# Convolution branches rotated over four column groups of TensorE, small products on three of them

## What is computed

```python
specs = [(w1, 0, 1), (w2, 6, 6), (w3, 12, 12), (w4, 18, 18)]        # weights, pad, dilation; w1 is 1x1, the others 3x3
branches = [_bn_relu(_conv(x, w, p, d), ...) for i, (w, p, d) in enumerate(specs)]   # 32 channels each
x_q = jnp.concatenate(branches, axis=1)
Q = einsum('oi,bihw->bohw', wq, x_q) + bq        # 16 rows
K = einsum('oi,bihw->bohw', wk, x) + bk          # 16 rows
V = einsum('oi,bihw->bohw', wv, x) + bv          # 128 rows
Qn = _l2n(Q).transpose(0, 2, 1)
Kn = _l2n(K)
tailor = 1.0 / (N + einsum('bnm,bm->bn', Qn, Kn.sum(-1) + EPS))
mat = einsum('bmn,bcn->bmc', Kn, V)
msum = V.sum(-1)[:, :, None] + einsum('bnm,bmc->bcn', Qn, mat)
out = gamma * (msum * tailor[:, None, :])
```

## Time and profile before

| | us |
|---|---|
| median of 3 runs | 16281.83 |
| lowest and highest | 16277.56, 16301.75 |
| the profiled execution | 16276.23 |
| its span | 16274.4 |
| PE busy in the span | 14161.2 (87%) |
| DVE, POOL, ACT busy | 13974.3, 13069.0, 10107.5 |
| mean granted clock of TensorE | 0.925 |

### The profile page before, as it was taken

The page is one execution under the profiler, slowest core; times in us unless marked ns, Lnnn a source line. Parts: engine busy times, 40 slices in busy tenths (PEclk is TensorE's granted clock), DMA queues, the critical chain, the costliest instruction groups (busy, mean ns, idle before and its releaser), DMA issues. The chain is left out here.

```text
span 16274.4 us, 144588 instructions
## 1 busy us (share of the span) xinstructions
PE 14161.2 (87%) x40704; PEld 5407.5 (33%) x40704; DVE 13974.3 (86%) x13537; ACT 10107.5 (62%) x14054; POOL 13069.0 (80%) x5647
## 2 busy tenths in 40 slices
PE   8999997888888888888888888888888888888886
PEld 3333332333333333333333333333333333333332
DVE  1222228999999999999999999999999999999997
ACT  2222225666666666666666666666666676666675
POOL 0000007999999999999999999999999999999996
PEclk9999998999999999999999999999999999999997
DMA  1111104444445545444455454454544444545544
GB/s 50 42 39 44 39 26 151 171 161 169 170 172 180 180 168 180 173 178 171 175 182 181 168 180 173 176 182 164 182 178 172 177 176 175 182 167 181 180 173 172
DMA packets 560359, 2505.37 MB, mean 154 GB/s; under 512 B 58695, under 2 KB 171063, under 8 KB 293448
## 3 DMA queue, kind: packets, MB, share of 16 engines
q1 hardware_dynamic: 549272, 2477.68, 42.9%
q10 hardware_dynamic: 10288, 18.44, 0.4%
HBM read 2325.32 MB, written 170.57 MB: 153 GB/s over the span
## 5 line engine op out<-in xcount | busy, mean ns | idle before, releaser
L794 POOL TENSOR_TENSOR hc<-h,c_all 128x1024 f32<-128x1024 f32 x4096 | 9531.7, 2359 | 574.0 <-DVE h L1161 496.1
L1031 PE MATMUL y_ps<-hc,ident 128*128 128x512 f32 x16392 | 8392.7, 664 | 1127.8 <-POOL hc L794 1127.6
L892 ACT ACTIVATE d_a<-dt,a_neg 128x512 f32<-128x512 f32 x8194 | 5596.1, 689 | 4081.4 <-DVE h L1161 4055.4
L1161 DVE TENSOR_TENSOR_SCAN h<-d_a,h,dbx_v 128x512 f32<-128x512 f32 x5456 | 6622.0, 1262 | 10.4 <-DVE dbx_v L1148 1.1
L1031 PEld LDWEIGHTS y_ps<-hc,ident 128*128 128x128 f32 x16392 | 3362.3, 211 | 6055.1 <-issue 4172.5
L1148 DVE TENSOR_TENSOR dbx_v<-dtx_ps,b_all 128x1024 f32<-128x1024 f32 x2816 | 3313.7, 1206 | 61.0 <-issue 26.2
L1161 DVE TENSOR_TENSOR_SCAN h<-d_a,h,dbx_p 128x512 f32<-128x512 f32 x2480 | 3027.7, 1262 | 10.8 <-issue 0.4
L783 POOL TENSOR_TENSOR dbx_p<-dtx,b_all 128x1024 f32<-128x1024 f32 x1280 | 3002.3, 2355 | 23.8 <-DVE h L1161 0.8
L480 POOL MEMSET ident_f<- 128x128 f32 x1 | 0.2, 205 | 2417.5 <-POOLq L45 2417.5
L273 PE MATMUL conv_ps<-image,w_taps 128*32 128x512 f32 x11520 | 1777.7, 594 | 0.0
L363 DVE RECIPROCAL k_inv<-k_nrm 128x4 f32<-128x4 f32 x256 | 45.5, 178 | 1774.2 <-ACT k_nrm L215 1774.2
(11 more groups left out here) (143 smaller groups left out, 9228.5 us busy)
## 6 DMA issues: line engine op xcount, KB each, us to landing
b_all<-bc_dram SPq DMA_DIRECT2D x1028, 1024.0 KB, 6.3
c_all<-bc_dram SPq DMA_DIRECT2D x1025, 1024.0 KB, 5.0
o_dram<-o_sb SPq DMA_DIRECT2D x257, 256.0 KB, 6.2
o_c<-o_dram SPq DMA_DIRECT2D x220, 256.0 KB
out<-r_c SPq DMA_DIRECT2D x220, 256.0 KB, 7.9
image<-in_x SPq DMA_DIRECT2D x91, 512.0 KB, 4.1
un<-un_dram SPq DMA_DIRECT2D x736, 34.0 KB
bc_dram<-low_bc SPq DMA_DIRECT2D x257, 64.0 KB, 4.6
```

What stands on the lines that cost most here:

```text
L794: nc.gpsimd.tensor_tensor(hc[:, n % HC], h[:, n], c_all[:, n // CG % 2, n % CG].unsqueeze(1).broadcast_to([128, 2, CH]), ALU.mult).then_in ...
L892: nc.scalar.activation(d_a[:, half], dt[:, p, half], ACT.Exp, scale=a_neg[:, half, n:n + 1]).then_inc(a_done, 1)
L1031: last = nc.tensor.matmul(y_ps[:, half], ident[:], hc[:, n % HC, half], start=False, stop=(n == S - 1))
L1161: nc.vector.tensor_tensor_scan(h[:, n, half], d_a[:, half], dbx, zero_col[:] if first else h[:, n, half, CH - 1:CH], ALU.mult, ALU.add).th ...
```

## The change

- The branches no longer have fixed column groups. Chunk r's 1x1 branch is on group r mod 4 and the dilated ones on the three groups behind it, in turn. Weights for the center are laid down twice in a row (8 x 32 columns), so that a window of it gives the turned order; the query weights and the batch norm's constants come in four turned copies.
- `query` is on group 0, `query_norm` on group 1, `outer` on group 2 (`small_ps` holds all three), and group 3 has none of them.
- The order of PE's work on an image is made by a planner (`batch`) when the kernel is built. It goes in rounds: in each, every group gets one matmul in turn (group 2 four outer products at once), a small product if it is due, or else its next tap. A tap's chunk may be up to three ahead of the oldest unfinished one. A center is put just before the first tap of its chunk, wherever in the round that is, and kv at the start of a round.
- `conv_ps` has four banks, `x_q` two; Q and its sum of squares have two each.
- ACT does relu of chunk k, norms of k+1, then `length` (root and stores) of k-2 and `query` (copy and square) of k-1.
- POOL clears only the margins of `image`; the first loads don't wait for the clearing. PE waits for each quarter of the first image, and for the last 24 rows of later ones at chunk 20.

```diff
-        conv_ps = ps("conv_ps", [128, 2, CH])
+        conv_ps = ps("conv_ps", [128, 4, CH])
         kv_ps = ps("kv_ps", [128, 2, CH])
-        mat_ps = ps("mat_ps", [KU, 2, CH])
-        qs_ps = ps("qs_ps", [128, CH])
-        s_ps = ps("s_ps", [128, CH])
+        small_ps = ps("small_ps", [128, 2, CH])
+        qs_ps, s_ps, mat_ps = small_ps[0:M], small_ps[32:64], small_ps[64:64 + KU]
...
-            sp.wait_ge(cleared, 6)
             for i in range(4):
                 rows = slice(i * 32, i * 32 + 32)
                 sp.dma_start(image[:, PAD + 32 * i:PAD + 32 * i + 32, PAD:PAD + W],
-                             t["x"][0, :, rows, :]).then_inc(x_loaded, 16)
-
+                             t["x"][0, :, rows, :]).then_inc(x_first[i], 16)
+
+            sp.wait_ge(cleared, CLEARED)
...
-        def loaded(eng, b):
-
-            eng.wait_ge(x_loaded, 16 * 4 + b * (16 * (PIECES - 2)))
+        def loaded(eng, b, r):
+
+            if b == 0:
+                for i in range(4):
+                    if r == max(0, (32 * i - max(DIL) - ROWS) // ROWS):
+                        eng.wait_ge(x_first[i], 16)
+            elif r == 0:
+                eng.wait_ge(x_loaded, 16 * b * (PIECES - 3))
+            elif r == ((PIECES - 3) * PIECE - max(DIL) - ROWS) // ROWS:
+                eng.wait_ge(x_rest, 16 * b)
...
-            pool.memset(image[:], 0.0).then_inc(cleared, 1)
+            pool.memset(image[:, 0:PAD], 0.0).then_inc(cleared, 1)
+            pool.memset(image[:, PAD:PAD + H, 0:PAD], 0.0).then_inc(cleared, 1)
+            pool.memset(image[:, PAD:PAD + H, PAD + W:WP], 0.0).then_inc(cleared, 1)
+            pool.memset(image[:, PAD + H:WP], 0.0).then_inc(cleared, 1)
...
+                norms(b * NCH)
+                for r in range(NCH):
+                    k = b * NCH + r
+                    relu(k)
+                    if r + 1 < NCH:
+                        norms(k + 1)
+                    if r >= 2:
+                        length(k - 2)
+                    if r >= 1:
+                        query(k - 1)
+                k = b * NCH + NCH - 1
+                length(k - 1)
+                query(k)
+                length(k)
...
+            def center(k, r):
+                if k >= 4:
+                    pe.wait_ge(bn_done, k - 3)
+                y0, turn = r * ROWS + PAD, (4 - r % 4) % 4 * BR
+                nc.tensor.matmul(conv_ps[:, k % 4], w_center[:, turn:turn + 4 * BR],
+                                 image[:, y0:y0 + ROWS, PAD:PAD + W], start=True, stop=False, skip_group_check=True)
+
+            def tap(k, r, n, group):
+                i = (group - r) % 4 - 1
...
+                while min(queries, norms, outers) < NCH:
+                    if (keyed < min(begun + 1, NCH, outers + 3) and now >= keys_at.get(keyed - 1, -far) + 5
+                            and (keyed < 3 or now >= done_at.get(keyed - 3, far) + 4)):
+                        loaded(pe, b, keyed)
+                        kv(b * NCH + keyed, keyed)
+                        keys_at[keyed] = now
+                        keyed += 1
+                    for g in range(4):
+                        if g == 0 and now >= done_at.get(queries, far) + 3:
+                            query(b * NCH + queries, queries)
+                            query_at[queries] = now
+                            queries += 1
+                        elif g == 1 and now >= max(query_at.get(norms, far), done_at.get(min(norms + 1, NCH - 1), far)) + 4:
+                            query_norm(b * NCH + norms)
+                            norms += 1
+                        elif g == 2 and now >= max(keys_at.get(outers, far), done_at.get(outers - 1, far) if outers else 0) + 6:
+                            for j in range(SUB):
+                                outer(b * NCH + outers, j)
+                            outers += 1
+                        elif waiting[g] and waiting[g][0][0] <= told + 3:
+                            r, n = waiting[g].pop(0)
+                            for c in range(begun, r + 1):
+                                if keyed <= c:
+                                    loaded(pe, b, c)
+                                center(b * NCH + c, c)
+                            begun = max(begun, r + 1)
+                            left[r] -= 1
+                            if left[r] == 0:
+                                done_at[r] = now
+                            ended = 0
+                            while told + ended < NCH and left[told + ended] == 0:
+                                ended += 1
+                            told += ended
+                            last = tap(b * NCH + r, r, n, g)
+                            if ended:
+                                last.then_inc(conv_done, ended)
+                    now += 1
```

More of the change, by code:

```diff
@@ L35 @@
 PIECES = H // PIECE
+CLEARED = 9
 HC = 4
@@ L329, in _ @@
+            for b in range(B):
+                batch(b)
         @block.vector
```

201 lines of the change are left out of this document (88 added, 113 removed).

## The result

Measured in turn on one chip: after 16401.2 us (median; 16390.4 to 16412.4), before 16286.0 us (16277.6 to 16301.8). The ratio is 1.0070, 95% interval 1.0052 to 1.0087: slower by 115 us. The forecast was +47, 16329 us, and its range ended at 16390. The direction held; the time is outside the range, and the slowdown is more than twice the forecast.

The account below looks back on a forecast made before the run. PE was taken to bound the first stage, busy 289.4 of the last image's 291.6 us. The terms gave +11.2 us per image, +90 for eight, and with the start +47: 16329 us, range 16236 to 16390.

Parts of the forecast that it names:

- Start: Before the first kv: less clearing and earlier loads let PE start at 14.0 instead of 56.89 us, -42.9 us once.
- Rounds: PE's rounds (one two-pass matmul per group) before the last chunk's kv: 223 instead of 245, -18.9 us per image.
- Interruptions: Switches to full-width matmuls and back: 57 instead of 32 per image, 0.17 to 0.27 us each, +5 us per image.
- Bursts and waits in the stream: Bursts: group 3's tap waits behind group 2's four outer products, +2.5 us per image; PE's waits for ACT and DVE, +11.6.
- (a): Centers of chunks 21, 25 and 29 wait for relu to free their bank: 1.04 us each, 3.1 per image.
- (b): The sum of squares waits for ACT's square, late by 0.3 to 0.5 us some seven times: 3.5 per image.
- (c): Between chunks 3 and 6 the query chain waits for DVE's denominators of the former image: 5 us per image.
- The end of an image: Last chunk's kv to next image's kv: 23.2 instead of 15.0 us, +9.1 with center 31 moved; low clock adds 1.9.
- free centers: Rival: a center in mid-round costs nothing, 17 rounds less per image, -14.6 us each, 16212 us in all; chance 0.09.
- no stream waits: Rival: ACT is ahead, so PE's waits in the stream don't come, -11.6 us per image, 16236 us; chance 0.13.
- The clock falls in the thin ends: Rival: at each image's end the clock falls 5 us earlier, +5.4 us per image, 16372 us; chance 0.22.
- Strict order: Rival: matmuls keep program order over all groups, outer products costing 25 instead of 2.5 us per image, 16509 us; chance 0.04.

Follow-up runs that it names:

- group3_first: The changed kernel with the planner's round visiting group 3 before groups 0, 1 and 2: 16290.1 us, ratio 0.9999.
- one_outer: The changed kernel with one of the four outer products per chunk (the last) instead of four: 16376.1 us, ratio 1.0053.
- late_bank: group3_first with a new chunk begun only two rounds after the last tap of the chunk whose bank it takes: 16269.7 us, ratio 0.9990.
- square_first: The changed kernel with ACT doing the query's copy and square before the older chunk's root and stores: 16367.5 us, ratio 1.0047.
- short_den: The changed kernel with DVE's denominator pieces cut to one of 128 columns each: 16351.8 us, ratio 1.0039.
- round_start: The changed kernel with centers only at a round's head, groups visited 3, 0, 1, 2, ACT's copy and square first, small products and keys respaced: 16138.2 us, ratio 0.9902.
- start_only: The kernel before with only the new start (margins cleared, early loads, PE waiting for each quarter of the first image): 16250.4 us, ratio 0.9973.
- flow_four: round_start planned over all 256 chunks, next image's work filling an image's end, four instead of two buffers for query copy and root: 16045.0 us, ratio 0.9853.
- split_pair: The kernel before with each chunk's center first and its kv only behind the first three taps: 16476.3 us, ratio 1.0117.
- square_four: square_first with four buffers instead of two for the query's copy and root: 16311.3 us, ratio 1.0016.

## Why the prediction was right in direction and wrong in size

By its own steps, per image:

- **Start**, -42.9 once: -42.7. Right.
- **Rounds**, -18.9: 245 to 223 by the same count in the trace, at 0.868 -19.1. Right, and group3_first shows that the mid-round centers are what keeps it from being more.
- **Interruptions**, +5: 57 instead of 32, the last kv included, at 0.285 each +7.1. The count of 25 more was right, the price too low. I had 0.17 to 0.27: the way back behind a kv (0.09) and the first pass behind a drain (0.10) can both be read in before, and I took only one of them at a time.
- **Bursts and waits in the stream**, +2.5 and +11.6, together 14.1: 18.6. **This is the step that failed.** Bursts 2.7 for 2.5 (one_outer); (a) 3.4 for 3.1 (late_bank); (b) 6.5 for 3.5 (square_first); (c) 2.8 for 5 (short_den). These add up to 15.4, but some 2 us of (b) and (c) are the same time in chunks 4 and 5, so that 3 to 5 of the 18.6 are in no single experiment. The mis-sized term is (b), the price of a late sum of squares: 5.1 alone (in the first image) to 6.5, against 3.5. I had counted how late ACT is (0.3 to 0.5, some seven times, 2.1 to 3.5, and took the upper end) and taken this as the price. The seven places are right, but a place costs 0.6 and more. As I read the rows, the price is what all four groups could have done while the stream stands: when the wait shows on PE, the groups have run dry one after the other, which no row counts as a wait. The term that I put at nothing is the second row of outer products that waits for DVE's addition of the first; square_first shows it, and its share of the 3 to 5 us is open. Round_start, which spreads the small products and starts chunks at the head of a round, has 3.7 us of excess in all. That the whole term was only 4.5 short is in part luck: (b) was too low by 1.6 to 3.0, (c) too high by 2.2.
- **The end of an image**, +9.1 and +1.9 for the clock: 15.1 to 24.7, +9.6, the center of chunk 31 before the last kv, +0.9, and the chunk behind the turn some 0.3 longer at clock 0.50: 10.8 for 11.0. Right, with the steps 3.8 to 3.9 apart as worked out. The forecast left out the stores that hold a copy by its two buffers; in after they show only 8.0 us in seven waits, in square_first 46.9.

Sum: -19.1 + 7.1 + 18.6 + 10.8 = 17.4, measured 17.5. So 6.3 us per image over the forecast, 50 us in eight images, of the 72 by which it missed: 4.5 per image from the excess and 2.1 from the interruptions, less 0.3 from the rest.

The other 22 us are no step of the change. The second stage of the profiled before took 13857.1 us; with the same code there it lies between 13857 and 13894 in the profiles of all kernels here but short_den, at 13883.1 in after. start_only, which leaves the stream of before as it was, has 13877.4. I had made the sum against one profile that lay at the low end, and added no spread for it. (From profile to median before gains 10 us, where the sum had 5.6, and after loses 1.) The time goes along with the mean granted clock of the execution: of the fifty executions of before beside these experiments, the five at 0.921 took 16296 us in the mean, the nine at 0.925 took 16278. The profiled before had 0.925, the profiled after 0.921, so that some 20 of the 26 us by which their second stages differ go with the clock. What sets it isn't settled, nor whether it is the cause.

Of the rivals, free centers are refuted (group3_first), and so are no stream waits (the waits of PE in after). The clock falls in the thin ends, but where the forecast put it, not 5 us earlier (1.00 until 944 us). Strict order is refuted (one_outer). Of the signs that the forecast named, the first kv (14.2 for 14), the waits before three centers (0.88 for 1.0) and the end of an image (24.7 for 23, 25 with the clock) came out; four late chunks took 38.8 us instead of 38, which is 0.2 per chunk and, over 31 chunks, the 6 us per image.

## What to carry to other kernels

Where matmuls of column groups share one instruction stream, count a wait by what the other groups lose while the stream stands, not by how late its operand is: here 1.4 us off ACT's chain gave 6.5 per image, 0.6 in a place where PE showed a wait of 0.2. Put full-width matmuls at the head of a round and keep two chunks' dependent small products out of one stretch (19 us of excess to 3.7 in round_start, with ACT's order and later steps besides). Before removing one wait, look at what the same engine or stream waits for next (stores by two buffers took back half of the gain, until there were four buffers). An image's end with dependent steps is best filled with the next image's work: flow_four is 1.5% faster than before, while the change as made is 0.7% slower.

## What the runs showed of the hardware

- Going from narrow to full-width matmuls and back costs 0.285 us (split_pair), in three pieces: 0.52 instead of 0.43 before, 0.10 on the first full-width pass, 0.09 on the way back.
- Order held within a column group only: in the earlier trace rows passes of two other groups start at 68.93, ahead of one of group 1 at 69.35 that stands before them in the program.
- A pause cost its own time and then the clock. After 5.29 us without a matmul (square_first), or gaps of 2.10 and 2.89 with two passes between them (after), the next pair of passes took 1.92 us (1.2 GHz level); in square_four, after 2.99 us, 1.05. The clock of after stayed at 0.50 for 3.5 us of the next image.
- Four column groups with four different moving inputs kept the pitch of three: 0.434 us per pass (a stretch of eight rounds on all four, from 2030.94 us in after, has no excess).
